# Quarter-array float32 products with the identity in place of full-array transpositions in a two-layer convolution kernel

## The reference

```python
# layer 0: 3x3 convolution with binary weights, sign(w) * alpha
x = x + _L0_conv_ref(_gn(x), L0_conv_weight, L0_conv_alpha)
# layer 1
def _L1_conv_ref(x, w_in, w_dw, fft_filt, w_out):
    h = jnp.einsum('oc,bchw->bohw', w_in, x)                  # 64 -> 256 channels
    hp = h.reshape(b, c, hh // P, P, ww // P, P).transpose(0, 1, 2, 4, 3, 5)
    f = jnp.fft.rfft2(hp.astype(jnp.float32)) * fft_filt      # 8x8 patches
    hp = jnp.fft.irfft2(f, s=(P, P))
    h = hp.transpose(0, 1, 2, 4, 3, 5).reshape(b, c, hh, ww)
    h = lax.conv_general_dilated(h, w_dw, (1, 1), 'SAME', feature_group_count=c, ...)
    x1, x2 = jnp.split(h, 2, axis=1)
    g = jax.nn.gelu(x1, approximate=False) * x2
    return jnp.einsum('oc,bchw->bohw', w_out, g)              # 128 -> 64 channels
x = x + _L1_conv_ref(_gn(x), ...)
```

## Time and profile before

| | |
|---|---|
| time, median of 3 runs | 5393.75 us (5391.17 to 5396.26) |
| time of the profiled execution | 5396.35 us |
| its span in the profile | 5394.6 us |
| PE busy | 5249.1 us, 97% |
| DVE, POOL, ACT busy | 4631.7 (86%), 4236.2 (79%), 3526.7 us (65%) |
| TensorE clock granted, mean | 0.997 |

### The profile page before, as it was taken

How to read it: one execution, slowest core, us unless ns; L and a number is a source line. 1 busy time by engine, 2 the same in 40 slices (tenths; PEclk the granted TensorE clock), 3 DMA queues, 4 the chain that set the end, 5 groups by cost and what they waited for, 6 DMA issues and landing times.

```text
span 5394.6 us, 200882 instructions
## 1 busy us (share of the span) xinstructions
PE 5249.1 (97%) x88932; PEld 3061.1 (57%) x88932; DVE 4631.7 (86%) x5701; ACT 3526.7 (65%) x4642; POOL 4236.2 (79%) x2503
## 2 busy tenths in 40 slices
PE   5999999999999999999999999999999999999998
PEld 4555555555555555555555555555555555555554
DVE  6889888898888888888898888988889888898886
ACT  3666666666666666666666676666666667666665
POOL 3878778787887877878778787887878878787787
PEclk9999999999999999999999999999999999999999
DMA  2011010110101101010010100101011110110000
GB/s 103 19 50 43 37 45 28 54 40 37 54 22 50 43 37 53 19 58 35 37 53 28 51 33 38 55 36 43 33 50 40 39 41 33 50 43 20 23 26 26
DMA packets 43804, 219.20 MB, mean 41 GB/s; under 512 B 5350, under 2 KB 5960, under 8 KB 36808
## 3 DMA queue, kind: packets, MB, share of 16 engines
q1 hardware_dynamic: 42952, 206.36, 9.9%
HBM read 103.58 MB, written 102.76 MB: 38 GB/s over the span
## 4 chain that ended last, share of the span: by engine, by line
PE 86%; DVE 10%; issue 3%; DMA 0%; ACT 0%; POOL 0%; DVEq 0%; SPq 0%; POOLq 0%; ACTq 0%
PE PS L913 28%; PE PS L931 21%; PE PS L873 14%; PE PS L901 12%; PE PS L945 7%; DVE v L670 5%; PE PS L882 4%; DVE hf L663 3%; DVE bn L601 1%; DVE g L695 1%; DVE PS L679 0%; DVE PS L686 0%; DMA alpha_sb<-in_alpha 0%; POOL v_lo L343 0%; PE PS L847 0%
## 5 line engine op out<-in xcount | busy, mean ns | idle before, releaser
L343 POOL TENSOR_TENSOR v_lo<-v,v_hi 128x1024 f16<-128x1024 f32 (+1 forms) x1792 | 3357.5, 1898 | 841.9 <-ACT v_hi L462 834.5
L462 ACT ACTIVATE v_hi<-v 128x1024 f16<-128x1024 f32 (+1 forms) x1792 | 1647.0, 944 | 902.4 <-DVE v L670 532.6
L670 DVE TENSOR_TENSOR v<-PS,smul 128x1024 f32<-128x1024 f32 (+1 forms) x1792 | 1909.8, 1086 | 288.6 <-PE PS L913 271.0
L913 PE MATMUL PS<-hf,c_nodes 64*64 64x512 f32 (+1 forms) x14336 | 1661.8, 556 | 25.7 <-DVE v L670 4.5
L931 PEld LDWEIGHTS PS<-c_ext,v_hi 128*128 128x128 f16 x14336 | 1129.9, 97 | 541.2 <-issue 198.5
L931 PE MATMUL PS<-c_ext,v_hi 128*128 128x100 f16 (+2 forms) x14336 | 1258.6, 203 | 5.2 <-ACT gel L482 3.8
L931 PE MATMUL PS<-c_ext,v_lo 128*128 128x100 f16 (+2 forms) x14336 | 1250.2, 202 | 0.0
L931 PEld LDWEIGHTS PS<-c_ext,v_lo 128*128 128x128 f16 x14336 | 1118.0, 97 | 1.2
L663 DVE TENSOR_TENSOR hf<-PS,mult 128x1024 f32<-128x1024 f32 (+1 forms) x896 | 955.0, 1086 | 117.5 <-PE PS L901 101.0
L901 PE MATMUL PS<-win_sb,xT 64*64 64x256 f32 x12544 | 824.9, 388 | 48.0 <-DVE hf L663 28.9
L873 PE MATMUL PS<-S_hi,csign 64*64 64x448 f16 (+2 forms) x8640 | 746.4, 336 | 9.2 <-POOL S_lo L336 9.2
(11 more groups left out here) (68 smaller groups left out, 4143.2 us busy)
## 6 DMA issues: line engine op xcount, KB each, us to landing
out_x<-Xa SPq DMA_DIRECT2D x96, 448.0 KB, 2.6
out_x<-Xb SPq DMA_DIRECT2D x96, 448.0 KB, 2.5
Xa<-in_x SPq DMA_DIRECT2D x8, 2240.0 KB, 9.0
Xb<-in_x SPq DMA_DIRECT2D x8, 2240.0 KB, 8.9
Xa<-in_x SPq DMA_DIRECT2D x8, 1792.0 KB, 7.0
Xb<-in_x SPq DMA_DIRECT2D x8, 1792.0 KB, 7.2
Xa<-in_x SPq DMA_DIRECT2D x8, 1344.0 KB, 6.0
Xb<-in_x SPq DMA_DIRECT2D x8, 1344.0 KB, 6.4
```

Of the source, the lines that this page charges most:

```text
L343: nc.gpsimd.tensor_tensor(v_lo[:, img, :, k0:k1, :], v32[:, V_ORDER[kind(b, s)][img].index(grp), :, 0:k1 - k0, :], v_hi[:, img, :, k0:k1, ...
L462: nc.scalar.activation(v_hi[:, img, :, k0:k1, :], v32[:, V_ORDER[kind(b, s)][img].index(grp), :, 0:k1 - k0, :], ACT.Copy).then_inc(act_vhi ...
L670: nc.vector.tensor_tensor(v32[:, V_ORDER[kind(b, s)][img].index(grp), :, 0:k1 - k0, :], PS[:, bank:bank + 2, 0:(k1 - k0) * C2].rearrange(" ...
L913: last = nc.tensor.matmul(PS[points, bank + side, 0:(k1 - k0) * C2], c_nodes[half, points], hf[half, img, k0:k1, :].rearrange("p k c -> p ...
```

## The change

The seven transpositions of a strip are replaced by 28 float32 products of quarters of the array: each takes 64 channels of one image and one patch of 64 pixels as the stationary operand, and a 64x64 quarter of the identity as the moving operand. Image `r` goes to bank `bank + r`, where before the seven blocks lay one behind the other over both banks, and ACT's copy reads in that order and writes the same `xT`.

```diff
@@ def pixels(n, s, bank)
-                nc.scalar.activation(xT[:].rearrange("p k c -> p (k c)"), flat(bank, NBLK * 128), ACT.Copy).then_inc(act_xT, 1)
+                nc.scalar.activation(xT[:].rearrange("p k (r c) -> p r k c", c=C),
+                                     PS[:, bank:bank + 2, 0:NBLK * C].rearrange("p r (k c) -> p r k c", c=C),
+                                     ACT.Copy).then_inc(act_xT, 1)
@@ def transposed(n, s, bank)
                 for k in range(NBLK):
-                    last = nc.tensor.transpose(flat(bank, NBLK * 128)[:, k * 128:(k + 1) * 128],
-                                               xn[:, 2 * k:2 * k + 2].rearrange("p q r c -> p (q r c)"), c_id[:])
+                    for r, side in ((0, 0), (1, 1), (0, 1), (1, 0)):
+                        last = nc.tensor.matmul(PS[side * P * P:(side + 1) * P * P, bank + r, k * C:(k + 1) * C],
+                                                xn[r * C:(r + 1) * C, 2 * k + side].rearrange("p r c -> p (r c)"),
+                                                c_id[r * C:(r + 1) * C, r * C:(r + 1) * C], start=True, stop=True)
                 last.then_inc(pe_xT, 1)
```

## The result

The changed kernel takes 5427.42 us (median of 4 runs, 5425.95 to 5431.66) against 5394.25 us before (4 runs). The ratio is 1.0063, 95% interval 1.005 to 1.0076: 33 us slower, where +7 was forecast and 5411 was the end of the range. The profiled execution has a span of 5426.5 us against 5394.6.

What follows compares the result with a forecast made beforehand. Plain steps were taken as bound by the turn's end plus ACT's copy, convolution steps by PE's own sequence. +8.0 and -0.6 us summed to +7.4, on 5393.75 giving 5401 us; range 5390 to 5411.

Steps and rivals of the forecast that it cites:

- The step that failed: PE's instruction fetch: 22,000 more instructions on 200,882, with fetch at 0.9% of the DMA engines, taken to cost nothing.
- Rival (B): Small products of the turn or their fetch cost more than L891's; at twice, +172 us, 5566; chance 0.04.
- The price in plain steps: 119 plain steps: turn ends 0.06 us later, ACT's copy takes 4 ns more; 118 x 0.068 = +8.0 us.
- L446's cost: ACT's copy of the turned patches, in the new order, takes 922 ns against 918, 4 ns more.
- The price in convolution steps: 105 convolution steps: block starts earlier, costs more, switch moves behind it; about -0.005 us each, -0.6 us in all.
- The three terms: Convolution step: -0.12 us earlier start, +0.06 for the block, +0.05 for the switch behind it; summed as about -0.005.
- Rival (A): Plain steps: the array switch removed behind the turn counts, -0.10 x 119 = -12 us, 5382; chance 0.05.
- Rival (E): Whole kernel faster by PE's clock; at 1.00 with transpositions and 0.997 in the mean, nothing left to win; chance 0.01.

Runs made afterwards that it cites:

- e5: The changed kernel with x loads of one row for each part from the third pair of images on; 5399.17 us (1.0008).
- e6: The kernel before with x loads of one row for each part from the third pair of images on; 5392.31 us (0.9997).
- e2: The changed kernel with quarter products in the 119 plain-step turns alone, convolution steps keeping transpositions; 5401.23 us (1.0009).
- e11: The changed kernel with quarter products in convolution steps alone and one-row x loads from the third pair of images on; 5396.76 us (1.0003).
- e7: The kernel before with plain-step turns by quarter products, moved ahead of the projection's second half; convolution steps by transpositions; 5397.88 us (1.0006).
- e4: The kernel before with its x loads cut from four a pair to seven of 0.4 to 1.3 MB; 5393.72 us (0.9997).
- e8: The kernel before with plain-step turns moved ahead of the projection's second half, all turns by transpositions; 5392.97 us (0.9996).
- e10: The kernel before with its loads of 2.2 and 1.8 MB made one of 4.0 MB; 5395.01 us (0.9999).
- e9: The changed kernel with 32 more products (128 PE instructions) in the prologue, shifting later code by half a fetched piece; 5426.88 us (1.0057).

## Why the prediction was wrong

- **The step that failed** is the last sentence of the bounds: "instruction fetch is 0.9% of the DMA engines, so I take it at nothing". The share is a mean, and the fetch's share of the DMA engines was never the question, but what stands ahead of one packet when PE needs it, and how long the 256 instructions before it last. It cost about 21 us in stalls and 4 in half clock behind them. Rival (B) named the fetch, but priced it as if every small product cost double (5566, with a chance of 0.04). The trace of before would have given the length of the fastest piece: 4.3 us for 256 instructions, 17 ns each, less the 98 that the denser turn pushes out of it, 1.6 us, makes 2.7 us, where 3.2 came. They would not have given the time lost.
- **The price in plain steps** was right: 0.82 + 0.22 - 0.98 to the later end of the turn, and the longer wait for ACT. L446's cost was not: it stayed at 917 ns. e5 minus e6 is 6.9 us against +7.4 (both kinds of step); e2 cost 5.2 against +8.0, with an interval from 0 to 10.
- **The price in convolution steps** was right as far as it can be told: -0.6 forecast; e11 leaves at most 1.6 us beside its waits. (The three terms as they are printed add up to -0.01 a step, -1 us, and not to -0.6; nothing hangs on it.)
- **The stalls come in convolution steps** because there the 56 pairs of the turn, 32 of `interpolated`, 8 of `evaluated` and 56 of `forward_transform` follow each other in less than 4 us (2057.22 to 2061, but for the stall). And SP issues the loads of 2.2 and 1.8 MB just ahead of them, while the convolution's matmuls run or within 1.5 us behind the last (1643.25, 1722.85, 1978.08, 2055.16), the two smaller ones of a pair in plain steps. In a plain step `forward_transform` starts 5.0 us behind the turn, and 16 matmuls of long `evaluated` products lie between: e2's fastest piece is 4.3 us. Rival (B) has the two blocks "in a plain step 4 us apart" and does not look at the other kind of step.
- **Rival (A)**, that the switch removed behind the plain turn would count, was rightly set low: the wait for ACT took it up, and e7 shows that it isn't to be had by reordering either.
- **Rival (E)**: a lower clock did play a part, on the other side: the changed kernel lost clock by its stalls.

What a page has on it stands apart. The Trainium skill, "Runtime: NRT & Kernel Launch", section "Instruction fetch mechanics", says that instructions are refilled in blocks of 16 KiB (256 instructions) while the current block runs, which the packets of 16,384 bytes and the stalls' places agree with. It also says that crossing a boundary is mostly hidden, which holds for all but 15 of the 802 here, and that the engine issues more slowly than the block fills; here PE took 3.2 us for a block and stood still up to 2.5 us, so there the measurement decides.

No version was found that beats the kernel before: e4, e7, e8 and e10 can't be told from it.

## What to carry to other kernels

When a change multiplies instructions, don't look at the mean share of the fetch: count how many instructions the engine starts while the longest transfers are under way, and compare that with the 256 of one fetched piece. A gap by "issue" in the middle of a block whose operands are ready, ended 1.4 us after a 16 KB instruction packet, was a fetch stall here; it is tested by making the loads around it small. A switch or a wait that a reordering removes must be followed to the next user of the same PSUM bank before it is counted as won.

## What the hardware showed that was not expected

- A PE piece of 256 instructions in 3.2 us is fed without a stall when the loads are of one row (e5). Behind 1.5 to 2.3 MB of loads PE was held up 15 times, by 1.1 to 2.5 us (changed kernel); behind output stores of 0.45 MB it stood idle for 0.9 to 1.2 us, four times (e11).
- The time from the landing of an instruction packet to the first instruction that goes on is 1.2 to 1.6 us at these stalls.
- Behind the three longest of the 15 stalls the granted clock was 0.50, 1.2 GHz, for 3.4 us; behind the others it stayed at 1.00, and so it did in e9 behind one of 2.4 us.
- Quarter products can start among the last products of the block before: four L885 began at 2056.94, ahead of the last L875 at 2057.03.
